# The gated layer's 257 keys as 128 + 128 + 1 in a six-stage Perceiver kernel

## What is computed

```python
h1 = jnp.einsum('eth,efh->etf', x, w1)        # x: layernorm of x, w1 = v1 = w2 = ctx_1024
h2 = jnp.einsum('eth,efh->etf', x, v1)
g = jax.nn.gelu(h1, approximate=False) * h2
return jnp.einsum('etf,efh->eth', g, w2)      # added to x
```

## Time and profile before

| | us |
|---|---|
| median of three runs | 2311.27 (2311.0 to 2311.86) |
| the profiled execution, its own time | 2309.65 |
| its span from first to last instruction | 2307.9 |
| mean granted PE clock | 0.966 |
| PE busy | 2119.3 (92%) |
| PE weight loads | 1563.2 (68%) |
| DVE busy | 1535.6 (67%) |
| ACT busy | 1300.8 (56%) |
| POOL busy | 1027.1 (45%) |

### The profile page before, as it was taken

One profiled execution on the slowest core, in us unless ns is written; L12 is line 12 of the kernel. 1 busy time (PEld: TensorE's weight loads), 2 busy tenths in 40 slices (PEclk: granted clock), 3 DMA queues, 4 the chain that ended last, 5 costly groups with the idle time before them and its releaser, 6 DMA issues. The chain is left out here.

```text
span 2307.9 us, 81023 instructions
## 1 busy us (share of the span) xinstructions
PE 2119.3 (92%) x27948; PEld 1563.2 (68%) x27949; DVE 1535.6 (67%) x5463; ACT 1300.8 (56%) x3747; POOL 1027.1 (45%) x935
## 2 busy tenths in 40 slices
PE   7989999997999899978999999999889999989994
PEld 4657777774677677756777777777556665665992
DVE  4578888874777743347888888888666666754442
ACT  3555555555888433336777777777645555532330
POOL 1024444333888300006555656555266666625115
PEclk9999999997999899988999999999999999979997
DMA  6640000000000000000111111111140000001112
GB/s 161 174 130 1 0 0 0 0 1 1 1 0 0 1 1 0 0 26 25 36 34 34 34 34 34 34 34 34 35 169 0 0 0 0 0 2 41 42 42 77
DMA packets 41208, 71.52 MB, mean 31 GB/s; under 512 B 6176, under 2 KB 30624, under 8 KB 40480
## 3 DMA queue, kind: packets, MB, share of 16 engines
q1 hardware_dynamic: 37792, 63.55, 9.4%
q0 software_dynamic: 3328, 6.82, 0.9%
HBM read 60.91 MB, written 9.44 MB: 30 GB/s over the span
## 5 line engine op out<-in xcount | busy, mean ns | idle before, releaser
L2276 ACT ACTIVATE xat_scores<-xat_scores,xat_least 128x257 f32<-128x257 f32 x512 | 258.5, 505 | 103.5 <-DVE xat_least L2410 102.3
L2410 DVE CUSTOM_DVE_ANT_0 xat_scores<-bank,xat_mask_b 128x257 f32<-128x257 f32 x512 | 207.6, 422 | 88.7 <-PE bank L2120 87.9
L1050 POOL TENSOR_TENSOR gqa_rnorm<-gqa_norm_min,gqa_minus_half 128x12 f32<-128x12 f32 x64 | 145.8, 2278 | 104.9 <-DVE gqa_norm_min L1127 104.9
L2178 PE MATMUL bank<-ident,xat_scores 128*128 128x128 f32 x1024 | 189.2, 287 | 0.0
L2178 PEld LDWEIGHTS bank<-ident,xat_scores 128*128 128x128 f32 x1024 | 116.4, 142 | 81.0 <-issue 49.0
L690 POOL TENSOR_TENSOR lin_q_softmax<-lin_q_exp,lin_q_rsum 128x512 f32<-128x512 f32 x64 | 66.7, 1042 | 223.2 <-DVE lin_q_rsum L751 223.2
L1693 DVE SCALAR_TENSOR_TENSOR X<-bank,expert_shares,X 128x128 f32 (+1 forms) x256 | 72.0, 343 | 130.9 <-PE bank L1607 130.7
L1630 ACT ACTIVATE moe_gelu<-bank 128x512 f32<-128x512 f32 x128 | 76.5, 597 | 146.1 <-PE bank L1597 146.1
L1607 PEld LDWEIGHTS bank<-moe_w,moe_gelu 128*128 128x128 f32 x1024 | 124.2, 192 | 30.8 <-issue 18.2
L1368 POOL TENSOR_TENSOR bat_scores<-bat_scores,bat_max 128x512 f32<-128x512 f32 x128 | 130.5, 1041 | 32.5 <-DVE bat_max L1400 32.5
L1400 DVE CUSTOM_DVE_ANT_0 bat_scores<-bank,bat_causal_add 128x128 f32<-128x128 f32 x512 | 110.7, 286 | 47.2 <-PE bank L1256 47.2
(11 more groups left out here) (320 smaller groups left out, 5826.9 us busy)
## 6 DMA issues: line engine op xcount, KB each, us to landing
glu_ctx_N<-in_ctxN SPq DMA_DIRECT2D x32, 576.0 KB, 4.3
xat_ctx_T<-in_ctxT SPq DMA_DIRECT2D x32, 516.0 KB, 3.6
xat_pad<-in_xat_pad SPq DMA_DIRECT2D x32, 128.5 KB, 3.4
expert_w<-in_glx_w SPq DMA_DIRECT2D x1, 4096.0 KB, 14.9
slot_rows<-gqa_zero_rows SPq DMA_DIRECT2D x1, 2560.0 KB, 11.0
slt_rows<-slot_rows SPq DMA_DIRECT2D x40, 64.0 KB, 1.8
slot_results<-slt_y POOLq DMA_DIRECT2D x40, 64.0 KB, 1.8
moe_w<-in_moe_w SPq DMA_DIRECT2D x2, 1024.0 KB, 5.8
```

The costliest lines, as they stand in the source:

```text
L1050: pool.tensor_tensor(rn[h][:, :], sm[h][:, :], half_neg[:, :], ALU.pow).then_inc(rnorm, 1)
L2178: m = pe.transpose(dst[:, c * P:(c + 1) * P], sx[j % 2][:, g, c * P:(c + 1) * P], k.ident[:, :])
L2276: act.activation(sx[j % 2][:, g, :], sx[j % 2][:, g, :], ACT.Exp, bias=mn[j % 2][g][:, 0:1], scale=-1.0, accum_out=sm[j % 2][:, g:g + 1]). ...
L2410: dve.tensor_tensor_reduce(sx[j % 2][:, g, :], pS[g][:, 0:J], mb[slot][:, j, :], 1.0, BIG, ALU.add, ALU.min, mn[j % 2][g][:, 0:1]).then_in ...
```

## The change

The 257 keys of a batch are two chunks of 128 and one single key.

- Loads: `ctxN` now has 128 partitions by 4 batches by 2 chunks. Three small arrays come ahead of X: the last keys of all 128 batches as rows (`lN`), the same laid out as 4 partitions by 32 tiles by 128 (`lR`), and a 4x128 matrix that puts batch b on its 32 rows (`eB`). X's groups 2 and 3 are loaded behind the four context tiles.
- At the start PE transposes `lN` and ACT copies it to `lT`. POOL puts the single key's four columns into `cT` for each tile (`put_last`), and h waits for that as well.
- Eight context transposes instead of twelve, two of gh instead of three; the copies and the gate have 256 or 257 columns.
- y: one product of `eB` with `lR` spreads the single key's rows over the tile, into the other columns of `pY`; then eight products instead of twelve. DVE multiplies the spread rows with the gate's last column and adds them to X in one instruction, and the add of y waits for it.
- `look_at(1)` stands behind gate(0), `look_at(2)` and `look_at(3)` behind the gates in DVE's bodies 3 and 4, ahead of the add. norm(4) waits for group 1 only, norm(8) for all.
- Eight tiles are written out at the front instead of four.

```diff
+            sp.dma_start(lN[:, :], ctx_last).then_inc(lasts_landed, 16)
+            sp.dma_start(lR[:, :, :], last_rows).then_inc(rows_landed, 16)
+            sp.dma_start(eB[:, :], batch_rows).then_inc(rows_landed, 16)
...
+            load_x(0)
+            load(0, 0)
+            load_x(1)
+            load(1, 1)
+            load(2, 2)
+            load(3, 3)
+            load_x(2)
+            load_x(3)
...
-                for c in range(NJ):
-                    m = pe.transpose(pC[b][:, c * JC:(c + 1) * JC], cN[slot][0:JC, b, c, :], k.ident[0:JC, 0:JC])
+                for c in range(NC):
+                    m = pe.transpose(pC[b][:, c * P:(c + 1) * P], cN[slot][:, b * NC + c, :], k.ident[:, :])
                 m.then_inc(c_turned, 1)
...
+                pe.wait_ge(last_put, t + 1)
                 wait(pe, gh_ready, t)
...
             def y(t, slot):
                 pe.wait_ge(gt_ready, t + 1)
                 wait(pe, added, 2 * (t - 1) + 1)
-                for c in range(NJ):
+                pe.matmul(pY[:, D:2 * D], eB[:, :], lR[:, t, :], start=True, stop=True)
+                for c in range(NC):
                     for b in range(BT):
                         o = c * P + b * S
                         m = pe.matmul(pY[b * S:(b + 1) * S, 0:D], gT[slot % 2][:, o:o + S],
-                                      cN[slot][0:JC, b, c, :], start=(c == 0), stop=(c == NJ - 1))
+                                      cN[slot][:, b * NC + c, :], start=(c == 0), stop=(c == NC - 1))
                 m.then_inc(y_ready, 1)
...
             def add(t, slot):
                 dve.wait_ge(y_ready, t + 1)
+                dve.scalar_tensor_tensor(out=k.X[:, t, :], in0=pY[:, D:2 * D], scalar=gh[slot % 2][:, LAST:J],
+                                         in1=k.X[:, t, :], op0=ALU.mult, op1=ALU.add).then_inc(last_added, 1)
+                dve.wait_ge(last_added, t + 1)
                 residual_tile(dve, k, t, pY[:, 0:D], added, 2 * t)
...
                     ctx_copy(t, slot, 1)
                     ctx_copy(t, slot, 3)
+                    gate(t, slot)
                     look_at(1)
-                    gate(t, slot)
-                if isinstance(t, int) and 1 <= t < 3:
-                    look_at(t + 1)
...
                 if nxt:
                     gate(*nxt)
+                if isinstance(t, int) and t in (3, 4):
+                    look_at(t - 1)
...
+            def put_last(t, slot):
+                wait(pool, h_ready, t - 1)
+                pool.tensor_copy(cT[slot % 2][:, :, LAST], lT[:, ts(t, BT)]).then_inc(last_put, 1)
```

More of the change, by code:

```diff
@@ L151, in _, with stage_ctx_glu @@
                 dve.tensor_tensor(dst[:, :], k.RSTD[:, :], k.MS[:, :], ALU.mult).then_inc(rc, 1)
-def stage_ctx_glu(nc, k, x, ident, ctxN, ahead):
-    JZ = NJ * JC
+def stage_ctx_glu(nc, k, x, ident, ctxN, ctx_last, last_rows, batch_rows, ahead):
+    NC, LAST = 2, J - 1
+    JF = NC * P
     with ExitStack() as ctx:
@@ L166, in stage_ctx_glu @@
         WAYS = 4
-        cN = [sb(f"ctx_N{i}", [JR, BT, NJ, D]) for i in range(WAYS)]
-        cT = [sb(f"ctx_T{i}", [P, BT, JZ]) for i in range(2)]
+        cN = [sb(f"ctx_N{i}", [P, BT * NC, D]) for i in range(WAYS)]
+        cT = [sb(f"ctx_T{i}", [P, BT, J]) for i in range(2)]
+        lN, lT = sb("last_N", [P, D]), sb("last_T", [P, P])
+        lR, eB = sb("last_rows", [BT, NT, D]), sb("batch_rows", [BT, P])
         xn = [sb(f"xn{i}", [P, D]) for i in range(2)]
         xT = [sb(f"xT{i}", [P, P]) for i in range(2)]
-        ge = [sb(f"gelu{i}", [P, JZ]) for i in range(2)]
-        gh = [sb(f"gh{i}", [P, JZ]) for i in range(2)]
-        gT = [sb(f"gh_T{i}", [JC, NJ * P]) for i in range(2)]
+        ge = [sb(f"gelu{i}", [P, J]) for i in range(2)]
+        gh = [sb(f"gh{i}", [P, J]) for i in range(2)]
+        gT = [sb(f"gh_T{i}", [P, NC * P]) for i in range(2)]
         pX, pG, pY, pH = k.bank[0], k.bank[5], k.bank[6], k.bank[7]
@@ L218, in tiles @@
         def tiles(eng, body):
-            for t in range(WAYS):
-                body(t, t)
-            with eng.Fori(0, NT // WAYS - 2) as i:
+            for t in range(2 * WAYS):
+                body(t, t % WAYS)
+            with eng.Fori(0, NT // WAYS - 3) as i:
                 for w in range(WAYS):
-                    body(WAYS * i + WAYS + w, w)
+                    body(WAYS * i + 2 * WAYS + w, w)
             for w in range(WAYS):
@@ L263, in g_transpose @@
                 wait(pe, gt_ready, t)
-                for c in range(NJ):
-                    m = pe.transpose(pG[0:JC, c * P:(c + 1) * P], gh[slot % 2][:, c * JC:(c + 1) * JC], k.ident[:, :])
+                for c in range(NC):
+                    m = pe.transpose(pG[:, c * P:(c + 1) * P], gh[slot % 2][:, c * P:(c + 1) * P], k.ident[:, :])
                 m.then_inc(g_turned, 1)
@@ L281, in body @@
                     pe.wait_ge(ident_landed, 16)
+                    pe.wait_ge(lasts_landed, 16)
+                    pe.transpose(pG[:, 0:P], lN[:, :], k.ident[:, :]).then_inc(lasts_turned, 1)
+                    pe.wait_ge(rows_landed, 32)
                     for b in range(BT):
@@ L322, in body @@
                 if isinstance(t, int) and t == 0:
+                    act.wait_ge(lasts_turned, 1)
+                    act.activation(lT[:, :], pG[:, 0:P], ACT.Copy).then_inc(lasts_copied, 1)
                     ctx_copy(t, slot, 0)
@@ L349, in norm @@
             def norm(t, slot):
-                if isinstance(t, int) and t in (0, 4):
-                    dve.wait_ge(rstd_done, 1 if t == 0 else len(GROUPS))
+                if isinstance(t, int) and t in (0, 4, 8):
+                    dve.wait_ge(rstd_done, {0: 1, 4: 2, 8: len(GROUPS)}[t])
                 wait(dve, turned, t - 1)
@@ L400, in _, with deviation @@
             pool.wait_ge(set_up, 1)
-            for g, (lo, hi) in enumerate(GROUPS):
+            def deviation(g):
+                lo, hi = GROUPS[g]
                 pool.wait_ge(means, hi)
@@ L405, in _, with body @@
                 pool.tensor_tensor(k.RSTD[:, lo:hi], k.SD[:, lo:hi], half_neg[:, lo:hi], ALU.pow).then_inc(rstd_done, 1)
+            def put_last(t, slot):
+                wait(pool, h_ready, t - 1)
+                pool.tensor_copy(cT[slot % 2][:, :, LAST], lT[:, ts(t, BT)]).then_inc(last_put, 1)
+            def body(t, slot):
+                nxt = after(t, slot, 1)
+                if isinstance(t, int) and t == 0:
+                    deviation(0)
+                    pool.wait_ge(lasts_copied, 1)
+                    put_last(t, slot)
+                if nxt:
+                    put_last(*nxt)
+                if isinstance(t, int) and t in (0, 4, 5):
+                    deviation({0: 1, 4: 2, 5: 3}[t])
+            tiles(pool, body)
 def unit(t, h):
@@ L2594, in layouts @@
     o["ctxT"] = ctx.reshape(NT, BT, JP, D).transpose(0, 3, 1, 2)
-    ctx_rows = np.zeros((NT, JR, BT, NJ, D), np.float32)
-    ctx_rows[:, :JC] = ctx.reshape(NT, BT, NJ, JC, D).transpose(0, 3, 1, 2, 4)
-    o["ctxN"] = ctx_rows
+    chunks, lasts = g["ctx_1024"][:, :J - 1].reshape(NT, BT, 2, P, D), g["ctx_1024"][:, J - 1]
+    o["ctxN"] = chunks.transpose(0, 3, 1, 2, 4).reshape(NT, P, 2 * BT, D)
+    o["ctx_last"], o["ctx_last_rows"] = lasts, lasts.reshape(NT, BT, D).transpose(1, 0, 2)
+    o["batch_rows"] = np.repeat(np.eye(BT, dtype=np.float32), S, axis=1)
     row = np.arange(P)
```

26 lines of the change are left out of this document (15 added, 11 removed).

## The result

The changed kernel takes 2324.58 us (median of four runs, 2323.56 to 2329.3), before 2311.14 in the runs beside it: a ratio of 1.0068, 95% interval 1.0054 to 1.0082. It is slower by 13.4 us between the medians and by 15.7 by the ratio; 14.5 were forecast. The profiled execution took 2324.8 us.

The account below looks back on a forecast made before the run. The prediction took a steady tile to be bound by a closed loop through DVE, not by PE. Start -1.5, 25 loops of 0.60 for +15.0 and end +1.0 gave +14.5, 2325.8 us, range 2318 to 2334.

Parts of the forecast that it names:

- The tile is a loop through DVE, not PE's stream: Steady gated-layer tile: a closed 3.35 us loop, 1.66 of it DVE's; at the high clock the change adds 0.60 us.
- Rival 1: Gated layer: PE is the bound, DVE's new work fits its idle time; -9 us, 2302; chance 4%.
- rival 2: Gated layer: even trade on PE, or half of DVE's addition hidden; within 4.6 us of before, 2311; chance 8%.
- The DVE instruction: 0.48: Between y and the copies: single-key instruction 0.344 us plus semaphore wait 0.14, together 0.48 us per tile on the loop.
- The spread product: 0.34, with 0.24 to 0.49: Head of y: the product spreading the single key's rows costs 0.34 us; with 0.22 gone from y, net +0.12.
- Transposes and the smaller gh: PE beside DVE's work: eight context transposes save 0.06 us, gh 0.11, worth nothing at the high clock.
- The start: Stage front up to h(6): later X and looks against an earlier clock rise, between -2.9 and no difference; -1.5 us taken.
- rival 3: Gated layer: clock rises much later or never; ten more low tiles +12 us, 2338, all of them +45; chance 8%.
- The end: +1.0: Behind the last h: add(30) and add(31) each grow by 0.48 us, +1.0 us together.

Follow-up runs that it names:

- the changed kernel with cut looks: Changed kernel with look_at(2) and (3), ten tiles of statistics each, cut into four pieces of five tiles in tiles 2 to 5; ratio to before 1.0059.

## Why the prediction was right

Point by point, against the steps of the prediction.

- *The tile is a loop through DVE, not PE's stream.* Right. Each addition to it showed in full (0.38 in before, 0.40 out of after, 0.41 both ways for the product), and the same work off it showed nothing (3.16 a tile with both off the loop, 3.22 with neither in the kernel). Rival 1 (PE is the bound) and rival 2 are out for the changed kernel: PE's idle time ahead of h rose to 0.8 (about 0.9 was forecast).
- *The DVE instruction: 0.48.* Measured 0.38 to 0.40. The instruction took its 0.35, but its wait on its own semaphore cost 0.03 behind it, not the 0.14 that the add's costs ahead of bn_stats. This term was 0.1 too large.
- *The spread product: 0.34, with 0.24 to 0.49.* Measured 0.41 to 0.42, in the upper half. With 0.22 gone from y the net is +0.19 to 0.20, not +0.12. The two misses cancel, which is luck: the terms now give +0.58, the 23 loops from h(8) to h(31) are longer by 0.58 each, the sixteen of the table by 0.62, and +0.60 was forecast. The Trainium skill, TensorEngine Tiling (Array Packing), "Key Properties", says that a change of tiling mode drains TensorE; it gives no price. I had taken it to mean my upper end of 0.49: the trace has 0.42 from this product to the products of 32 columns behind it, so the rule agrees in kind, and my reading of it was too dear.
- *Transposes and the smaller gh are worth nothing at the high clock.* Right: they lie in PE's idle time. The eight transposes of the changed kernel step by 0.115 (75.75 to 76.68 ahead of gh), so they save nothing over twelve at 0.078 (0.93 against 0.94 us).
- *The start.* h(1) 16.98 (17.3 forecast), h(2) 22.78 (22.3), h(6) 43.56 against the 42.9 to 45.6 between which I took the middle: -2.2 where -1.5 was forecast. The value was near, the reason only half right. I had the clock rise once and then hold, "with far more idle time than here". It rose early, at 23, fell at 37, and was back only at 51. That is the step that failed, and a small piece of rival 3 came in its place. The low stretch went on past h(6): the two tiles to h(8) took 10.2 us where two at 4.0 would have been 8.0, so the 25 loops from h(6) came to 17.0 us more, not 15.0: 3.6 in these two, 13.4 in the 23 behind them.
- *The end: +1.0.* From the last h to the next stage it is 8.59 instead of 7.55: +1.04.

The sum at the next stage was to be +14.5 and is 153.99 - 138.17 = +15.8; behind it the two traces stand 14.3 to 18.0 us apart, with a clock that changes at other times, and end 15.2 apart; the medians differ by 13.4. So the 14.5 came out as near as it did with some luck: the start, the loops and the end together made 1.3 more than forecast, and the distance between the medians is 1.8 less than that between the traces.

Not settled is what makes the clock fall inside this layer. A long standstill is not needed; why the same kernel has one fall more in one trace than in another is open as well; that PE's share of work in a tile matters is argued from the stretches above and was not tried by itself.

## What to carry to other kernels

Before an instruction is priced, close the loop of one steady tile from the timeline, start to start, and see whether the new instruction stands on it: DVE was busy for 58% of the loop before and PE for 91%, and a DVE instruction of 0.35 us in the wrong place cost its full price, while in its idle time ahead of the gate it cost nothing. The same holds for the product on PE, the "busier" engine. An edit that looks bad as a whole (here +13 us) can be a good one (-0.17 us a tile without the single key's work in y and the add) with two instructions in the wrong place; with these moved the next stage starts 8.7 us earlier than before, not 16 to 18 later.

## What the runs showed of the hardware that I had not expected

- Code of one engine that shifts by a few instructions can cost time in a far-off loop, by all signs because it loads code at every turn: 101 transfers on queue 14 instead of 35 to 38, DVE idle for 3.1 and 1.7 us per turn, PE at the low clock behind it, 79 us in all, in one of the two kernels taken away by sixteen idle memsets. Before an edit is judged by its total, compare that row of the page.
- An f32 product of four partitions costs 0.41 us between a full-width transpose and products of 32 columns, as much as nearly four steps of y, and 0.72 at the low clock.
- The granted clock can fall with no pause of PE longer than 1.6 us (the changed kernel with cut looks, at 33 and 47 us), and in one trace of the changed kernel it fell in the steady loop, at 68 us, with none longer than 1.14.
